# A graph network's first layer: its dense stages joined into one wave of fifteen steps over ten chunks

## The chip, the cores and the metric

The kernel runs on one core of a Trainium2 chip. The metric is the device time of one execution in microseconds; lower is better. A core has TensorE (PE; PEld is its weight load), VectorE (DVE), ScalarE (ACT), GpSimd (POOL), and DMA queues fed by SyncE (SP) and GpSimd.

## The reference, cut to what matters

Four graph layers follow each other on 5000 nodes of 128 features and 80000 edges, all in fp32. The change is in the first layer, which runs three times over the same weights:

```
for _ in range(3):
    att = _gat(x, src, dst, edge_attr, ...)          # edge attention: q(x[dst]), k and v (x[src]+edge_attr), softmax per node
    att = _ln(att @ w_ao.T + b_ao + x, ln1_g, ln1_b)
    inter = gelu(att @ w_int.T + b_int)              # 128 -> 512
    m = _ln(inter @ w_out.T + b_out + att, ln2_g, ln2_b)
    gi, gh = m @ w_ih.T + b_ih, h @ w_hh.T + b_hh
    r, z = sigmoid(ir + hr), sigmoid(iz + hz)
    n = tanh(inn + r * hn)
    h = (1.0 - z) * n + z * h
    x = _ln(h, ln3_g, ln3_b)
```

## The kernel before

State lies transposed in SBUF: features on the 128 partitions, 5120 padded nodes along the row, worked on in `CHUNKS` = 10 chunks of 512. The program is a list of blocks; in a block each engine has its own instruction list, in order, tied to the others by semaphores, and a block ends when all engines have ended. The first layer is a hardware loop over three iterations. In each: `node_rows` (L717 to L759) turns the state back into rows (4 transposes a chunk), stores them to `table_x` in DRAM and makes the queries in `t1`; `gat_score_pass`, `gat_softmax` and `gat_value_pass` go over the edges; then six dense blocks follow, each over all ten chunks before the next begins:

- `from_rows` (attention output): VectorE divides the sums by the softmax totals (L1520 to L1529), TensorE transposes (L1567), ScalarE copies, TensorE multiplies with `w_ao` (L1573), VectorE adds bias and residual (L1547).
- `layer_norm`, three times: TensorE sums over partitions with a matrix of ones (L624), VectorE centres (L686), ScalarE squares (L657), TensorE sums the squares by 128 columns against one column of ones (L631), ScalarE takes the root (L661), VectorE inverts (L691), TensorE spreads the result by transposes (L640), VectorE multiplies (L694), ScalarE applies gain and shift (L670). It works in two turns of five chunks and one root for each turn.
- `feed_forward`: four expansion products (L1587), Gelu on ScalarE (L1607), four contraction products in one bank (L1593), bias and residual on VectorE (L1614).
- `gru` (the gated update): six products a chunk (L1633 to L1636), two sigmoids (L1644, L1645), two VectorE steps (L1656, L1659), tanh (L1649), three more VectorE steps (L1663 to L1667).

ScalarE keeps its functions in tables; where the next function is in another table the compiler puts an ACT_TABLE_LOAD ahead of it. `clear_block` is an empty block that clears the semaphores before the loop goes round.

Of the kernel before, what the change touches and what calls it, by code (L numbers as in the profile page):

```python
# [17 lines left out]
F32 = mybir.dt.float32  # L18
I32 = mybir.dt.int32
ALU = mybir.AluOpType  # L20
ACT = mybir.ActivationFunctionType
AX_X = mybir.AxisListType.X

P = 128
N, E, D = 5000, 80000, 128
TILES = E // P
BLOCKS = -(-N // P)
# [25 lines left out]
Q_W = D + 4  # L53
CHUNK = 512
CHUNKS = NP // CHUNK
U = 5
BIG = 1.0e38
GAT_HEADS, GAT_ITERS, GAT_FF = 4, 3, 4
# [5 lines left out]
def bank4(ap):  # L64
    return ap.rearrange("p (a b) -> p a b", b=P)


def program(nc, io, out):
    ctx = ExitStack()
    with ctx:  # L70
        def sb(name, shape, dt=F32, where=ctx):
            return where.enter_context(nc.sbuf_tensor(name, shape, dt))

        def sems(*names):
            return [ctx.enter_context(nc.semaphore(n)) for n in names]
# [4 lines left out]
        @contextmanager  # L80
        def block(name, *used):
            with nc.Block(name) as b:  # L82
                cleared = [s for s in spent if s not in used]
                assert len(cleared) == len(spent), name
                spent.clear()

                @b.sync
                def _(sp):
                    for s in cleared:
                        sp.sem_clear(s)  # L90
                yield b
            spent.extend(used)

        def clear_block(name):
            with block(name):
                pass


        table_x = nc.dram_tensor("table_x", [NP, D], F32)
# [10 lines left out]
        ident = sb("ident", [P, P])  # L110
        iota_row = sb("iota_row", [P, P])
        ones = sb("ones", [P, P])
        (WK, WV, WQ, WAO, WINT, WOUT, GIH, GHH, GIN1, GIN2, WEDGE, GGIH, GGHH, NW) = (
            0, 1, 2, 3, 4, 8, 12, 15, 18, 19, 20, 24, 27, 30)
        wt = sb("wt", [P, NW, P])
        w3 = sb("w3", [P, 8, P])
# [10 lines left out]
        gate_bias = sb("gate_bias", [P, 2, 2])  # L127
        eps_col = sb("eps_col", [P, 1])
        blank = sb("blank", [1, P])
        bq_rows = sb("bq_rows", [P, D])  # L130
        bk_rows = sb("bk_rows", [P, D])
        bv_rows = sb("bv_rows", [P, D])
# [17 lines left out]
        hT = sb("hT", [P, NP])  # L150
        resT = sb("resT", [P, NP])
        t1 = sb("t1", [P, ACC_BLOCKS * Q_W])
        states = sb("states", [P, NP + ACC_BLOCKS * ACC_W])
        xT, acc = states[:, 0:NP], states[:, NP:]
        psum = ctx.enter_context(nc.psum_tensor("psum", [P, 8, CHUNK], F32))
# [4 lines left out]
        def wcol(name, k=0):  # L160
            return vec[:, VEC[name] + k:VEC[name] + k + 1]
# [4 lines left out]
        with ExitStack() as tmp:  # L166
# [25 lines left out]
            with block("constants", s_load, s_load2, s_const, s_wt, s_wcopy, s_xl, s_rows) as b:  # L192
                @b.sync
                def _(sp):
                    for to, of in loads[0::2]:
                        sp.dma_start(to, of).then_inc(s_load, 16)
# [342 lines left out]
        def at_least(eng, sem, value):  # L539

            if not (isinstance(value, int) and value <= 0):
                eng.wait_ge(sem, value)  # L542
# [27 lines left out]
        def acc_rows(c, lo, n):  # L570

            return acc[:, bass.ds(c * (4 * ACC_W), 4 * ACC_W)].rearrange("p (b w) -> p b w", w=ACC_W)[:, :, lo:lo + n]
# [5 lines left out]
        V = 2  # L578
# [23 lines left out]
        select = sb("select", [P, REGIONS, GROUP, P])  # L602
# [100 lines left out]
        r_stored = sems(*(f"rows_stored{u}" for u in range(V)))  # L703
# [126 lines left out]
        score = sb("score", [P, STEPS, GAT_HEADS])  # L830
# [745 lines left out]
        def feed_forward(name, src, dst, function, w_in, b_in, w_out, b_out):  # L1576
# [41 lines left out]
        g_product, g_gated, g_reset, g_new, g_read, g_step = sems(  # L1618
            "gru_products", "gru_gates", "gru_reset_applied", "gru_new", "gru_banks_read", "gru_step")

        def gru(name, msg, h, w_ih, w_hh, gates, b_in, b_hn):

            with ExitStack() as tmp:
                gate = sb(f"{name}_gate", [P, V, 2, CHUNK], F32, tmp)
                new = sb(f"{name}_new", [P, V, CHUNK], F32, tmp)
                with block(name, g_product, g_gated, g_reset, g_new, g_read, g_step) as b:
# [26 lines left out]
                    def _(dve):  # L1653
# [13 lines left out]
                            dve.tensor_tensor(h[:, cols(c)], new[:, u, :], gate[:, u, 0, :], ALU.add).then_inc(g_step, 1)  # L1667
                        pairs(dve, reset, update)

        b_stats, b_root, b_applied, b_scale, b_done = sems("bn_step", "bn_rooted", "bn_applied", "bn_product", "bn_done")  # L1670

        def batch_norm(name, src, gain, shift, dst=None, residual=None, weight=None, bias=None):
# [123 lines left out]
        def parts_of(w, first, count):  # L1796
            return [w[:, first + k, :] for k in range(count)]


        layer_norm("l0_norm", resT, xT, LN_EPS, also=hT)  # L1800
        with nc.Fori(0, GAT_ITERS) as it:
            node_rows("l0_rows", xT, queries=True)
            gat_score_pass("l0_scores", [it * ROWS] * REGIONS)
            gat_softmax("l0_softmax")
            gat_value_pass("l0_values")
            from_rows("l0_attention", t1, heads=GAT_HEADS, eps=1e-16, offset=bv_rows[:], weight=wt[:, WAO, :], bias=wcol("b_ao"), residual=xT)
            layer_norm("l0_ln1", t1, xT, 1e-12, wcol("ln1_g"), wcol("ln1_b"))
            feed_forward("l0_ffn", xT, t1, ACT.Gelu, parts_of(wt, WINT, GAT_FF), [wcol("b_int", k) for k in range(GAT_FF)],
                         parts_of(wt, WOUT, GAT_FF), wcol("b_out"))
            layer_norm("l0_ln2", t1, xT, 1e-12, wcol("ln2_g"), wcol("ln2_b"))  # L1810
            gru("l0_gru", xT, hT, parts_of(wt, GIH, 3), parts_of(wt, GHH, 3), gate_bias[:, 0, :], wcol("b_ih", 2), wcol("b_hh", 2))
            layer_norm("l0_ln3", hT, xT, 1e-12, wcol("ln3_g"), wcol("ln3_b"))
            clear_block("l0_end")
        add_state("l0_residual", xT)

# [57 lines left out]
```

## Time and profile before

| | us |
|---|---|
| median of 3 runs | 12100.61 (12093.36 to 12107.19) |
| the profiled execution | 12019.95 |
| its span | 12018.1 |
| busy in the span: TensorE, VectorE, ScalarE, GpSimd | 6550.1, 4612.7, 2251.5, 6209.6 |
| one iteration of the first layer, second | 1754.6 |
| its six dense stages, in the first | 256.7 |
| granted TensorE clock, mean | 0.734 |

The profile is of one execution, taken on the chip. A granted clock of 1 is 2.4 GHz for TensorE, of 0.5 it is 1.2 GHz. Busy times of engines overlap; what counts for a stage is the engine or the chain of waits that ends last in it. A row of the windows view has, in this order: the stretch, its length, the busy time and instructions of PE, PEld, DVE, ACT and POOL, the granted clock, the DMA share and GB/s. A row of the view by line has: busy us, mean ns of one, idle before, and what ended it.

### The profile page before, as it was taken

The numbers are of one execution on the slowest core, as the hardware profiler recorded it, in microseconds if no ns is written. First come the engines' busy times: TensorE is split into PE (matmuls) and PEld (weight loads), VectorE is DVE, ScalarE is ACT, GpSimd is POOL, SyncE is SP. The second block draws the span as 40 slices with busy tenths as digits, with TensorE's granted clock in tenths as the row PEclk, the third lists the DMA queues.
The fourth block names the chain that finished last, engine by engine and source line by source line (L and its number), as shares of the span: only waits on it lengthen the run. The fifth ranks groups of instructions, "written<-read, shape, count | busy, mean of one in ns | idle before, by whom it ended". The sixth has DMA issues, their size and how long they took to land. (4 is left out here: it accounts for less than half of the span.)

```text
span 12018.1 us, 148393 instructions
## 1 busy us (share of the span) xinstructions
PE 6550.1 (55%) x36272; PEld 5479.0 (46%) x36273; DVE 4612.7 (38%) x10118; ACT 2251.5 (19%) x4313; POOL 6209.6 (52%) x6365
## 2 busy tenths in 40 slices
PE   3666786566786665884335334433533443365555
PEld 3555665555765555853323223233323322244443
DVE  4444754444754444752113112211311221135555
ACT  1222552222542222641000000000000000011111
POOL 2666423666414665504663665466366456625553
PEclk6777898777897777996667666666766666677777
DMA  2444322444313443401111111211111121112221
GB/s 75 128 127 127 103 64 69 128 127 125 106 42 88 129 128 105 125 22 42 46 45 61 46 46 36 68 45 46 60 45 45 34 71 46 46 43 77 78 77 55
DMA packets 698434, 894.29 MB, mean 74 GB/s; under 512 B 148417, under 2 KB 443211, under 8 KB 698130
## 3 DMA queue, kind: packets, MB, share of 16 engines
q0 software_dynamic: 198368, 429.61, 13.6%
q1 hardware_dynamic: 498474, 461.96, 12.4%
q8 instruction: 51, 0.84, 0.0%
q14 instruction: 125, 1.02, 0.0%
q10 hardware_dynamic: 1416, 0.86, 0.0%
HBM read 698.72 MB, written 193.14 MB: 74 GB/s over the span
## 5 line engine op out<-in xcount | busy, mean ns | idle before, releaser
L857 POOL DMA_INDIRECT states<-table_typed,tile_idx x2512 | 2415.9, 962 | 1777.8 <-issue 721.2
L840 POOL DMA_INDIRECT states<-table_x,src_idx x2016 | 1980.1, 982 | 1862.7 <-POOLq L82 742.8
L979 PE MATMUL psum<-states,l_sums_select 128*128 x4480 | 905.5, 336 | 1729.7 <-issue 1696.3
L979 PEld LDWEIGHTS psum<-states,l_sums_select 128*128 128x128 f32 x4480 | 777.0, 244 | 1854.3 <-issue 1853.8
L961 DVE SCALAR_TENSOR_TENSOR l_sums_select<-dst_all,pair_start,iota_row 128x512 f32<-128x512 f32 x560 | 402.1, 749 | 2212.5 <-remote 1401.0
L1091 PE MATMUL psum<-ident,select 128*128 128x128 f32 x2016 | 418.3, 344 | 1199.3 <-DVE states L1059 723.4
L840 POOL DMA_INDIRECT l_pass_ring<-table_kv,src_idx x672 | 655.1, 975 | 658.9 <-DVE score L1312 286.3
L1068 DVE TENSOR_TENSOR states<-w,psum 128x512 f32<-128x512 f32 x504 | 345.2, 685 | 1544.0 <-ACT w L1048 969.0
L857 POOL DMA_INDIRECT states<-table_x,tile_idx x628 | 602.1, 959 | 626.2 <-POOLq L82 337.0
L979 PE MATMUL psum<-states,select 128*128 x2240 | 469.4, 348 | 808.8 <-issue 769.4
L944 ACT COPY t<-psum 128x512 f32<-128x512 f32 x50 | 29.3, 585 | 4534.1 <-PE psum L979 2586.3
L1091 PEld LDWEIGHTS psum<-ident,select 128*128 128x128 f32 x2016 | 297.9, 178 | 1263.5 <-DVE states L1059 567.3
L979 PEld LDWEIGHTS psum<-states,select 128*128 128x128 f32 x2240 | 404.7, 254 | 876.7 <-issue 876.0
L1144 POOL TENSOR_TENSOR w<-iota_row,dst_local 128x512 f32<-128x512 f32 x504 | 524.3, 1041 | 459.7 <-ACT select L1161 459.7
L1108 PE MATMUL psum<-t,l_scores_spread 128*128 x4032 | 675.2, 317 | 72.1 <-issue 71.6
L1105 PE MATMUL psum<-wt,l_scores_mixT 128*128 128x128 f32 x4032 | 713.5, 336 | 0.0
L1105 PEld LDWEIGHTS psum<-wt,l_scores_mixT 128*128 128x128 f32 x4032 | 672.1, 252 | 0.6 <-issue 0.2
L1108 PEld LDWEIGHTS psum<-t,l_scores_spread 128*128 128x128 f32 x4032 | 630.4, 233 | 75.8 <-issue 75.7
L961 DVE SCALAR_TENSOR_TENSOR select<-dst_all,pair_start,iota_row 128x512 f32<-128x512 f32 x280 | 200.2, 749 | 1035.7 <-remote 567.1
L1231 PE MATMUL psum<-l_values_msg,select 128*128 128x132 f32 x4032 | 549.5, 279 | 68.2 <-DVE l_values_msg L1171 68.2
L1048 ACT COPY w<-psum 128x512 f32<-128x512 f32 x504 | 300.5, 596 | 1355.7 <-remote 844.0
L1220 PE MATMUL psum<-wt,l_values_ring 128*128 128x128 f32 x4032 | 535.7, 277 | 15.4 <-DMA l_values_ring<-rows_dram 15.4
(357 smaller groups left out, 11997.4 us busy)
## 6 DMA issues: line engine op xcount, KB each, us to landing
states<-in_edge_attr_dram SPq DMA_DIRECT2D x2016, 64.0 KB
rows_dram<-l_scores_mixT SPq DMA_DIRECT2D x504, 256.0 KB
l_values_ring<-rows_dram SPq DMA_DIRECT2D x504, 256.0 KB
table_typed<-l_rows_rows SPq DMA_DIRECT2D x40, 1024.0 KB, 4.3
states<-table_typed,tile_idx POOLq DMA_INDIRECT x2512
states<-table_x,src_idx POOLq DMA_INDIRECT x2016
l_pass_ring<-table_kv,src_idx POOLq DMA_INDIRECT x672
table_x<-l_rows_rows SPq DMA_DIRECT2D x40, 256.0 KB, 2.3
```

The lines of the kernel that those rows point to most:

```text
L840: pool.indirect_dma_start(out=ring[:, k % REGIONS, u, :], out_offset=None, in_=table, in_offset=at).then_inc(gathered[k % REGIONS], 16)
L857: pool.indirect_dma_start(out=ring[:, k % TILE_RING, u, :], out_offset=None, in_=table, in_offset=at).then_inc(gathered[k % REGIONS], 16)
L961: dve.scalar_tensor_tensor(out=picked(k), in0=dst_all[:, bass.ds(column, GROUP)].unsqueeze(2).broadcast_to([P, GROUP, P]), scalar=pair_sta ...
L979: ins = pe.matmul(to, picked(k)[:, u, :], rows, start=False, stop=True, skip_group_check=True)
L1048: act.copy(key[:, r % 2, :, :], keys(r)).then_inc(p_evacuated, 1)
L1068: dve.tensor_tensor(prod.rearrange("p (a b) f -> p a b f", a=2), key[:, r % 2, :, :].rearrange("p (a b) f -> p a b f", a=2), queries(r)[:, ...
L1091: pe.transpose(psum[:, 0, u * P:(u + 1) * P], select[:, r, u, :], ident[:])
L1105: pe.matmul(keys(r)[:, u, :], mixT[:, r, u, :], wt[:, WK, :], start=True, stop=True)
L1108: ins = pe.matmul(queries(r)[:, u // pair, u % pair, :], spread[:, r % 2, u, :], q, start=True, stop=True)
L1144: pool.tensor_tensor(away[:, r % 2, :, :], iota_row[:].unsqueeze(1).broadcast_to([P, GROUP, P]), dst_local[:, bass.ds(step_of(i, r), GROUP ...
L1220: ins = pe.matmul(values(r)[:, u, :], ring[:, r, u, :], wt[:, WV, :], start=True, stop=True)
L1231: ins = pe.matmul(sums(r, u), select[:, r, u, :], msg[:, r, u, :], start=True, stop=True)
```

## The change

One block, `dense_chain`, takes the place of the six dense blocks and of `node_rows` in the loop. Its fifteen stages (TURN to NEXT) have fixed lags; in slot t a stage works on chunk t minus its lag, and there are 24 slots. All engines write their list out slot by slot, the latest stages first. What an engine has in a slot waits for the other engines' part of the same chunk, made in an earlier slot or this one. Each norm takes its root for one chunk at a time, into four columns. The three sums share bank 2, the spreads bank 4, the expansion and the gates banks 5 and 6. The expansions alternate between those two banks. The last stage, NEXT, is the rows and queries of the following iteration, so `node_rows` runs once ahead of the loop, with a `clear_block` of its own, and the third iteration makes rows that nobody reads.

The diff, with the helpers `here` (run a stage if its chunk exists), `due` (how many chunks a stage has done by slot t) and `reached` (wait if not yet waited for) and the other stages' bodies left out, and the stages' common indentation cut:

```diff
+            TURN, PRODUCT, SUM, VAR, SPREAD, EXPAND, CONTRACT, UPDATE, NEXT = 0, 1, (2, 7, 11), (3, 8, 12), (4, 9, 13), 5, 6, 10, 14
+            SLOTS = CHUNKS + NEXT
...
+            def next_rows(t, c):
+                reached(c_written[2], c + 1)
+                reached(c_mixed, due(t - 1, TURN))
+                reached(c_att, due(t - 1, PRODUCT))
+                reached(g_read, due(t - 1, UPDATE))
+                for k in range(4):
+                    pe.transpose(psum[:, 0, k * P:(k + 1) * P], xT[:, part(c, k)], ident[:])
+                for k in range(4):
+                    ins = pe.matmul(psum[:, 1, k * P:(k + 1) * P], xT[:, part(c, k)], wt[:, WQ, :], start=True, stop=True)
+                ins.then_inc(c_next, 1)
+            def summed(t, n, c):
+                reached((c_att, c_fed, g_step)[n], (c + 1) * (3 if n == 2 else 1))
+                for m in range(3):
+                    reached(c_centred[m], due(t if m > n else t - 1, SUM[m]))
+                pe.matmul(psum[:, 2, :], ones[:], norm_in(n, c), start=True, stop=True).then_inc(c_summed[n], 1)
+            def varied(t, n, c):
+                reached(c_squared[n], c + 1)
+                for m in range(3):
+                    reached(c_rooted[m], due(t - 1, VAR[m]))
+                for k in range(4):
+                    ins = pe.matmul(var_at(n, c, k), sq[n][:, c % 2, k * P:(k + 1) * P], ones[:, 0:1], start=True, stop=True)
+                ins.then_inc(c_varied[n], 1)
+            def spread(t, n, c):
+                reached(c_inverse[n], c + 1)
+                for m in range(3):
+                    reached(c_normed[m], due(t if m > n else t - 1, SPREAD[m]))
+                for k in range(4):
+                    ins = pe.transpose(psum[:, 4, k * P:(k + 1) * P], std[:, n, c % 2, k:k + 1].broadcast_to([P, P]), ident[:])
+                ins.then_inc(c_spread[n], 1)
+            def contract(c):
+                reached(c_fed, c)
+                for k in range(GAT_FF):
+                    reached(c_bent, GAT_FF * c + k + 1)
+                    ins = pe.matmul(psum[:, 7, :], wt[:, WOUT + k, :], inner[:, c % 2, k, :], start=k == 0, stop=k == GAT_FF - 1)
+                ins.then_inc(c_contracted, 1)
+            def gates_of(t, c):
+                reached(c_query, due(t, NEXT))
+                reached(c_att, due(t - 1, PRODUCT))
+                reached(g_read, c)
+                pe.matmul(psum[:, 1, :], wt[:, GHH + 2, :], hT[:, at(c)], start=True, stop=True)
+                reached(c_bent, GAT_FF * due(t - 1, EXPAND))
+                reached(g_gated, c)
+                for k in range(2):
+                    pe.matmul(psum[:, 5 + k, :], wt[:, GHH + k, :], hT[:, at(c)], start=True, stop=False)
+                reached(c_written[1], c + 1)
+                for k in range(2):
+                    pe.matmul(psum[:, 5 + k, :], wt[:, GIH + k, :], msg[:, c % 2, :], start=False, stop=True)
+                reached(c_next_copied, due(t, NEXT))
+                reached(c_mixed, due(t - 1, TURN))
+                pe.matmul(psum[:, 0, :], wt[:, GIH + 2, :], msg[:, c % 2, :], start=True, stop=True).then_inc(g_product, 1)
...
+            def expand(t, c):
+                reached(c_written[0], c + 1)
+                reached(g_gated, due(t, UPDATE))
+                for k in range(GAT_FF):
+                    reached(c_bent, GAT_FF * c + k - 1)
+                    pe.matmul(psum[:, 5 + k % 2, :], wt[:, WINT + k, :], att_in[:, c % 3, :], start=True, stop=True).then_inc(c_expanded, 1)
...
+            for t in range(SLOTS):
+                here(t, NEXT, next_rows, t)
+                here(t, SPREAD[2], spread, t, 2)
+                here(t, SUM[2], summed, t, 2)
+                here(t, CONTRACT, contract)
+                here(t, SUM[1], summed, t, 1)
+                here(t, SPREAD[1], spread, t, 1)
+                here(t, UPDATE, gates_of, t)
+                for n in (2, 1, 0):
+                    here(t, VAR[n], varied, t, n)
+                here(t, SPREAD[0], spread, t, 0)
+                here(t, SUM[0], summed, t, 0)
+                here(t, PRODUCT, attention, t)
+                here(t, EXPAND, expand, t)
+                here(t, TURN, turn, t)
+        @b.scalar
...
+            def gates_of(c):
+                act.wait_ge(g_product, c + 1)
+                at_least(act, g_step, 3 * c)
+                act.activation(gate[:, 0, :], psum[:, 5, :], ACT.Sigmoid, bias=gate_bias[:, 0, 0:1])
+                act.activation(gate[:, 1, :], psum[:, 6, :], ACT.Sigmoid, bias=gate_bias[:, 0, 1:2]).then_inc(g_gated, 1)
+                act.wait_ge(g_read, c + 1)
+                act.activation(new, new, ACT.Tanh, bias=wcol("b_ih", 2)).then_inc(g_new, 1)
+            def root(t, n, c):
+                for m in range(3):
+                    at_least(act, c_varied[m], due(t, VAR[m]))
+                at_least(act, c_spread[n], c - 1)
+                act.activation(std[:, n, c % 2, :], psum[:, 3, (n * 2 + c % 2) * 4:(n * 2 + c % 2) * 4 + 4], ACT.Sqrt,
+                               bias=eps_t[:], scale=1.0 / D).then_inc(c_rooted[n], 1)
+            def bend(c):
+                at_least(act, c_contracted, c - 1)
+                for k in range(GAT_FF):
+                    act.wait_ge(c_expanded, GAT_FF * c + k + 1)
+                    act.activation(inner[:, c % 2, k, :], psum[:, 5 + k % 2, :], ACT.Gelu, bias=wcol("b_int", k)).then_inc(c_bent, 1)
...
+            for t in range(SLOTS):
+                here(t, NEXT, next_copy)
+                here(t, SPREAD[2], written, 2)
+                here(t, SUM[2], square, 2)
+                here(t, SUM[1], square, 1)
+                here(t, SPREAD[1], written, 1)
+                here(t, UPDATE, gates_of)
+                for n in (2, 1, 0):
+                    here(t, VAR[n], root, t, n)
+                here(t, SPREAD[0], written, 0)
+                here(t, SUM[0], square, 0)
+                here(t, EXPAND, bend)
+                here(t, TURN, mix)
+        @b.vector
...
+            def feed(c):
+                dve.wait_ge(c_contracted, c + 1)
+                at_least(dve, c_centred[1], c - 1)
+                dve.scalar_tensor_tensor(out=fed[c % 2], in0=psum[:, 7, :], scalar=wcol("b_out"), in1=att_in[:, c % 3, :],
+                                         op0=ALU.add, op1=ALU.add).then_inc(c_fed, 1)
+            def make_rows(c):
+                at_least(dve, c_turned, c - 1)
+                at_least(dve, c_rows, c)
+                to = rows[:, c % 2, :].rearrange("p (b h e) -> p b h e", b=4, h=GAT_HEADS)
+                total = acc_rows(c, D, GAT_HEADS)
...
+            def update(c):
+                dve.wait_ge(g_new, c + 1)
+                dve.tensor_tensor(gate[:, 0, :], hT[:, at(c)], new, ALU.subtract).then_inc(g_step, 1)
+                dve.wait_ge(g_step, 3 * c + 1)
+                dve.tensor_tensor(gate[:, 0, :], gate[:, 0, :], gate[:, 1, :], ALU.mult).then_inc(g_step, 1)
+                dve.wait_ge(g_step, 3 * c + 2)
+                dve.tensor_tensor(hT[:, at(c)], new, gate[:, 0, :], ALU.add).then_inc(g_step, 1)
...
+            make_rows(0)
+            for t in range(SLOTS):
+                here(t, NEXT, query)
+                here(t, SPREAD[2], normed, 2)
+                here(t, SUM[2], centred, 2)
+                here(t, CONTRACT, feed)
+                here(t, SUM[1], centred, 1)
+                here(t, SPREAD[1], normed, 1)
+                here(t, NEXT, query_bias)
+                if t + 1 < CHUNKS:
+                    make_rows(t + 1)
+                here(t, UPDATE, reset)
+                here(t, SPREAD[0], normed, 0)
+                for n in (2, 1, 0):
+                    here(t, VAR[n], inverse, n)
+                here(t, SUM[0], centred, 0)
+                here(t, UPDATE, update)
+                here(t, PRODUCT, attended)
+            dve.memset(t1[:, BLOCKS * Q_W:], 0.0)
+        @b.sync
+        def _(sp):
+            for c in range(CHUNKS):
+                sp.wait_ge(c_next_copied, c + 1)
+                sp.dma_start(table_x[at(c), :].rearrange("(b p) f -> p b f", p=P), bank4(rows_out[:, c % V, :])).then_inc(r_stored[c % V], 16)
+            for stored in r_stored:
+                sp.wait_ge(stored, 16 * (CHUNKS // V))
...
         layer_norm("l0_norm", resT, xT, LN_EPS, also=hT)
+        node_rows("l0_rows", xT, queries=True)
+        clear_block("l0_start")
         with nc.Fori(0, GAT_ITERS) as it:
-            node_rows("l0_rows", xT, queries=True)
             gat_score_pass("l0_scores", [it * ROWS] * REGIONS)
             gat_softmax("l0_softmax")
             gat_value_pass("l0_values")
-            from_rows("l0_attention", t1, heads=GAT_HEADS, eps=1e-16, offset=bv_rows[:], weight=wt[:, WAO, :], bias=wcol("b_ao"), residual=xT)
-            layer_norm("l0_ln1", t1, xT, 1e-12, wcol("ln1_g"), wcol("ln1_b"))
-            feed_forward("l0_ffn", xT, t1, ACT.Gelu, parts_of(wt, WINT, GAT_FF), [wcol("b_int", k) for k in range(GAT_FF)],
-                         parts_of(wt, WOUT, GAT_FF), wcol("b_out"))
-            layer_norm("l0_ln2", t1, xT, 1e-12, wcol("ln2_g"), wcol("ln2_b"))
-            gru("l0_gru", xT, hT, parts_of(wt, GIH, 3), parts_of(wt, GHH, 3), gate_bias[:, 0, :], wcol("b_ih", 2), wcol("b_hh", 2))
-            layer_norm("l0_ln3", hT, xT, 1e-12, wcol("ln3_g"), wcol("ln3_b"))
+            dense_chain("l0_dense")
             clear_block("l0_end")
         add_state("l0_residual", xT)
```

## Rows read from the trace of the kernel before

**Rows 1.** Windows of the first iteration: attention, norm 1, feed-forward, gated update, gap, rows stage.

```profile
1664.90:1697.90 33.00, 19.98 (x60) 10.03 (x60) 29.16 (x60) 5.56 (x10) 0.00 (x0) 0.77 0.00 0
1698.20:1727.90 29.70, 26.27 (x140) 19.53 (x140) 13.95 (x23) 15.85 (x23) 0.00 (x0) 0.82 0.00 1
1727.90:1799.30 71.40, 70.41 (x160) 30.96 (x160) 7.49 (x10) 28.76 (x41) 0.00 (x0) 0.98 0.00 0
...
1829.10:1889.60 60.50, 53.43 (x120) 23.31 (x120) 33.86 (x50) 20.58 (x31) 0.00 (x0) 0.93 0.00 0
...
1921.60:1927.20 5.60, 0.00 (x0) 0.00 (x0) 0.03 (x1) 0.00 (x0) 0.00 (x0) 0.55 0.05 10
1927.20:1957.40 30.20, 17.31 (x120) 15.83 (x120) 23.46 (x41) 5.85 (x10) 0.00 (x0) 0.90 0.29 88
```

**Rows 2.** Timeline of TensorE, merged: start, us, what, count, idle before.

```profile
1698.20 4.53 PE L624 MATMUL psum<-t,ones 128*128 128x512 f32 x10 [1.11 <-PEq L82]
...
1706.95 6.24 PE L624 MATMUL psum<-t,ones 128*128 128x512 f32 x10
...
1714.15 2.40 PE L640 MATMUL psum<-ident,l_ln_std 128*128 128x128 f32 x20 [0.97 <-DVE l_ln_std L691]
...
1733.01 3.60 PE L1593 MATMUL psum<-l_ffn_inner,wt 128*128 128x512 f32 x8
...
1889.91 6.99 PE L624 MATMUL psum<-hT,ones 128*128 128x512 f32 x10 [7.31 <-PEq L82]
...
1910.56 4.53 PE L631 MATMUL psum<-ones,l_ln_sq 128*128 128x1 f32 x40
```

**Rows 3.** ScalarE's groups by line, first iteration: count, busy us, mean ns, idle before.

```profile
L1607 ACT ACTIVATE l_ffn_inner<-psum,vec 128x512 f32<-128x512 f32 x40 | 27.5, 687 | 39.0 <-PE psum L1587 39.0
L670 ACT ACTIVATE states<-states,vec 128x512 f32<-128x512 f32 x30 | 22.8, 807 | 9.9 <-DVE states L694 9.6
L657 ACT ACTIVATE l_ln_sq<-states 128x512 f32<-128x512 f32 x30 | 18.8, 630 | 33.2 <-DVE states L686 33.2
L1649 ACT ACTIVATE l_gru_new<-l_gru_new,vec 128x512 f32<-128x512 f32 x10 | 7.2, 720 | 4.6 <-DVE l_gru_new L1659 4.6
L1644 ACT ACTIVATE l_gru_gate<-psum,gate_bias 128x512 f32<-128x512 f32 x10 | 6.9, 687 | 31.9 <-PE psum L1636 31.9
L661 ACT ACT_TABLE_LOAD x3 | 3.8, 1283 | 0.1
L661 ACT ACTIVATE l_ln_std<-psum,l_ln_eps 128x20 f32<-128x20 f32 x6 | 1.7, 277 | 10.3 <-PE psum L631 10.3
```

**Rows 4.** VectorE's groups by line, the same stretch.

```profile
L686 DVE SCALAR_TENSOR_TENSOR states<-psum,t 128x512 f32<-128x512 f32 x20 | 13.8, 691 | 17.4 <-PE psum L624 17.4
L1614 DVE SCALAR_TENSOR_TENSOR t<-psum,vec,states 128x512 f32 (+1 forms) x10 | 7.5, 751 | 65.0 <-PE psum L1593 65.0
L691 DVE RECIPROCAL l_ln_std<-l_ln_std 128x20 f32<-128x20 f32 x6 | 1.6, 272 | 10.0 <-ACT l_ln_std L661 10.0
```

**Rows 5.** Timeline: two hops, a square before a load, two loads and what follows.

```profile
1699.33 0.69 DVE L686 SCALAR_TENSOR_TENSOR states<-psum,t 128x512 f32<-128x512 f32 x1 [1.04 <-PE psum L624]
...
1700.12 0.63 ACT L657 ACTIVATE l_ln_sq<-states 128x512 f32<-128x512 f32 x1 [4.58 <-DVE states L686]
...
1703.49 0.63 ACT L657 ACTIVATE l_ln_sq<-states 128x512 f32<-128x512 f32 x1 [0.23 <-DVE states L686]
1704.14 1.28 ACT L661 ACT_TABLE_LOAD   x1
...
1727.96 1.28 ACT L1607 ACT_TABLE_LOAD   x1 [0.27 <-PEq L82]
1730.08 0.69 ACT L1607 ACTIVATE l_ffn_inner<-psum,vec 128x512 f32<-128x512 f32 x1 [0.84 <-PE psum L1587]
```

**Rows 6.** Windows of two us: after a variance stretch, and in an idle of TensorE.

```profile
1886.00:1888.00 2.00, 0.00 (x0) 0.00 (x0) 1.93 (x4) 0.25 (x1) 0.00 (x0) 0.50 0.00 0
...
1708.00:1710.00 2.00, 2.00 (x3) 0.78 (x3) 0.69 (x1) 0.40 (x1) 0.00 (x0) 0.50 0.00 0
```

More of the change, by code:

```diff
@@ L1668, in _ @@
                         pairs(dve, reset, update)
+        c_rows, c_turned, c_mixed, c_product, c_att, c_link = sems(
+            "att_rows", "att_turned", "att_mixed", "att_product", "att_done", "att_rows_step")
+        c_summed, c_centred, c_squared, c_varied, c_rooted, c_inverse, c_spread, c_normed, c_written = (
+            sems(*(f"norm{n}_{what}" for n in range(3)))
+            for what in ("summed", "centred", "squared", "varied", "rooted", "inverse", "spread", "normed", "written"))
```

133 lines of the change are left out of this document (added).

## The prediction, made before the changed kernel was run

> **What bounds the kernel now.** I read the windows first, cut at the stage borders of the first iteration of layer 0 [rows 1]. From 1664.9, the end of the value pass, to the last norm's end at 1921.6 is 256.7 us; after 5.6 us for block ends, clear and loop, the rows stage takes 30.2, and then the next pass starts. GpSimd is idle in all of it, so only TensorE, VectorE and ScalarE can set its length. The feed-forward stage has TensorE busy 70.4 of 71.4 us at clock 0.98, and the gated update is near that; the attention and rows stages are held by VectorE (29.2 of 33.0, 23.5 of 30.2); the norms, of which one row stands for three, lie between, at clock 0.82. So the region is mostly TensorE-bound already; the longest waits in it are VectorE's for a contraction, 65.0 us [rows 4], and are cover rather than loss. Idle of other engines is no gain to be had.
>
> **TensorE's own work, the floor.** At 2.4 GHz a 512-column product is two passes of 0.43: ten passes take 4.53, eight (a contraction or an expansion) 3.43 to the next start [rows 2]. Twenty transposes take 2.40, so four 0.48; forty variance passes 4.53, so a chunk 0.90. Per chunk: product and three sums 4 x 0.86 = 3.4; expansion and contraction 6.9; six gate products 5.15; variances 2.7; four groups of transposes 1.9; next rows and queries about 1.3 (17.3 busy us for ten chunks, part at half clock [rows 1]). That is 21.4, or 214 us for ten. Against 256.7 + 30.2 = 286.9 now, perfect overlap would save 73 us an iteration.
>
> **What the wave costs, slot by slot.** All three engines go in written order, so a slot lasts as long as the longest round trip in it, not as long as TensorE's sum. Durations: Gelu, square and sigmoid 0.69, 0.63, 0.69, tanh 0.72, norm output 0.81, root 0.28 [rows 3]; a 512-column VectorE operation 0.69, feed 0.75, reciprocal 0.27 [rows 4]; a hop between engines 0.1 to 0.3: two passes begun at 1698.20 end at 1699.06, VectorE starts at 1699.33, ScalarE 0.10 behind it [rows 2, 5]. Roots, Gelu and sigmoid each come behind a table load of 1.28 [rows 3]. Now five loads serve an iteration. In the wave roots run in slots 3 to 21, Gelu in 5 to 14, sigmoid in 10 to 19, and ScalarE goes sigmoid, roots, Gelu in each: 35 loads. The load is not held by the wait behind it: it starts 0.02 after the last square and runs while the products that the root waits for go on [rows 5]. So the sigmoid's load hides under the products; those of the roots (from slot 10) and of Gelu stand on the round trip.
>
> Slots 0 to 5: VectorE bounds. make_rows is three full operations and two small ones of at most a reciprocal's length with their gaps, 2.55; centring, norm, inverse and attended add up to 2.4. By slot 5 its end is at 26.4; then square, load 1.28, Gelu, and since banks 5 and 6 alternate, expansions 2 and 3 only behind Gelu 0. Slot 5 ends at 30.7.
>
> Slots 6 to 9: contraction 3.43, feed to 4.46 behind it (and centring of norm 1), make_rows behind feed to 7.0, norm, inverse, centring to 8.7, square, load to 10.7, Gelu 0 to 11.4, two expansions 1.8, turn 0.5: 13.6. With the second norm's work 14.1, 14.6, 14.6. These are at 87.6.
>
> Slots 10 to 14: contraction, sum, transposes, gates: 9.9 to the gates' end. From there: sigmoids to 1.5, reset to 3.0, tanh 3.7, sqrt load 5.0, roots 5.8, inverse and centring 7.0, square 7.7, Gelu load 9.0, Gelu 0 9.7, two expansions 11.45. TensorE has 2.7 + 0.5 + 0.9 + 1.7 to do beside it and then stands about 4 us. With the sum, transposes and next rows that precede the next contraction (0.86, rising to 2.7) the slots are 22.2, 22.2, 21.5, 22.8, 22.2. At 198.5.
>
> Slots 15 to 19: no expansion, but norm 2's sum waits for the update, and VectorE does the update behind the inverses: 3.7 + 1.28 + 0.8 + three operations = 8.0 after the gates' end. So 17.9, 16.3 (the second sum waits for the first's centring), 14.5, 14.5, 13.9: at 275.6. Slots 20 to 23 and the last store: sum, centring, square, variance, root, inverse, transposes, norm, output, next rows, copy, DMA: 11.6. The whole, at full clock: 287.
>
> **The clock.** Ten 512-column passes take 4.53 us normally, 6.24 after a variance stretch and 6.99 after 7.3 us of idle [rows 2]; the granted clock is 0.50 in both places [rows 6], the lower of its two levels. A restart thus costs 1.7 to 2.5. Slots 16 to 20 begin after a gap as long as that: 5 x 2.5 = 12.5. Slots 10 to 14 have 2.7 us of variances and then the gap, but also 10 us of dense products: 0 to 1.7 each, I take 0.9, 4.5. Slots 1 and 5: 3. So 20, with bounds 5 (only half the late gaps count) and 45 (every slot from 5 on pays 2.5 or more). A chain is 307 to 308 us.
>
> **The rest.** Queries, their bias, copies and stores of next rows run in slots 14 to 23 beside the above; the queue of SP issues ten stores as before, 14 us apart, then 4, so ScalarE's copy does not wait for them. The third iteration makes next rows nobody reads; that is in its 11.6. Clearing and looping behind the chain replaces the 5.6 ahead of the rows stage, so they cancel. The rows stage ahead of the loop is the first iteration's own; the extra clear block is no row of its own, between 0 and the whole 5.6: I take 3. The three passes are untouched. Code written out straight already runs in the norms without a fetch gap in forty of them [rows 2], so 0.
>
> **The sum.** Goes: 3 x 256.7 + 2 x 30.2 = 830.5. Comes: 3 x 308 + 3 = 927. Difference +96.5. The profiled execution took 12019.95 (span 12018.1); the median of the runs is 12100.61, 80.66 higher, and I add the difference to that: 12197 us. The chain would have to be under 275.8 to pay. With the clock's bounds (292 and 333) and the hand-made round trips off by 10, likeliest case alone: 12120 to 12300.
>
> **The rivals.** *TensorE sets the slots (faster).* If neighbouring slots overlap better than I trace, the slots from 6 on last as long as TensorE's sum: 214 less 18 done before, plus 30.7 to get there and 8 to drain, is 235; 3 x 235 + 3 - 830.5 = -122, so 11978. For it: feed-forward and update now keep TensorE at 97 and 88% busy [rows 1]. Against it: there the two engines trade within one kind of work with no load between; here Gelu of a slot cannot start before the roots of the same slot. It decides once 32 of the 73 us from 308 down to 235 are gone. 0.18.
>
> *Nothing to see.* The clock costs nothing and the round trips are about ten us shorter, chain 268 to 284: within 24 us of 12101, which is the 0.2% that a measurement of this kernel can tell from no change. 0.12.
>
> *A switch of table costs more than its load.* After the load at 1727.96 the first Gelu starts 0.84 late, for which its product is an explanation too [rows 5]; if that were drain, some 20 loads an iteration stand on the path (slot 5 to 9 one, 10 to 14 two, 15 to 19 one): 17 us each, 50 in all, 12247. 0.10.
> The Trainium skill speaks against this change here: "ScalarE: Activation LUTs", section What ACT_TABLE_LOAD costs, gives 1283 ns plus about 1380 of drain for every switch, and its section on table sets asks for calls to be batched by set. The trace agrees with the 1283; of the drain it shows 0.02 before the load and at most 0.84 behind it. By the page's figure the sum would be 83 us longer, an estimate of 12280.
>
> *The clock stays low (slower still).* If every slot from 15 on ran wholly at 1.2 GHz (36 us of products on the path doubled, not 12.5 added) and slots 10 to 14 lost 5 each, the chain is 352: 12330. The attention stage speaks for it (TensorE busy 20 of 33 us, clock 0.77), the rows stage against it (17 of 30, clock 0.90) [rows 1]. 0.10.
>
> **The numbers.** My forecast holds 0.50, the two slower rivals 0.20, no change 0.12, faster 0.18. So slower 0.70, same 0.12, faster 0.18. Range for eight in ten: up to 12310, where most of the low-clock case is outside; down to 12020, part way into the faster case. Likeliest: 12197.
>
> **What the next profile would show.** Some 35 table loads an iteration, thirty or so of them more than now; TensorE idle 3 to 5 us in each of slots 10 to 14 with expansion 2 waiting for Gelu; 7 or 8 us between gates in slots 15 to 19 with the sum waiting for VectorE's update; slots of 14, 22 and 15 us; a chain of about 308, mean clock 0.8 or so. Wrong would be: ScalarE ahead of its products, slots of 18 us in the middle, or a chain under 276.

## The result, and where the time went

The changed kernel takes 12154.92 us (median of five runs, 12147.31 to 12166.59), the one before on the same chip 12100.61: a ratio of 1.0046, 95% interval 1.0031 to 1.0061, slower by 54 us (37 to 74). Forecast was 12197, range 12020 to 12310. Direction and range held, and so did the mechanism in the main (each slot waits for a round trip through ScalarE's table loads); the loss was forecast 42 us too large.

Two views of the profile after: the first lines of the page, and ScalarE's groups of table loads over the whole span, three iterations.

```profile
span 12152.2 us, 148055 instructions
PE 6604.6 (54%) x36392; PEld 5527.7 (45%) x36393; DVE 4627.7 (38%) x10195; ACT 2376.3 (20%) x4485; POOL 6206.1 (51%) x6365
...
L1872 ACT ACT_TABLE_LOAD x45 | 57.7, 1283 | 0.8
L1879 ACT ACT_TABLE_LOAD x30 | 38.5, 1283 | 0.5
L1863 ACT ACT_TABLE_LOAD x30 | 38.5, 1283 | 0.6
```

L1872 is the root, L1879 Gelu, L1863 the sigmoid: 105 loads, 35 an iteration, where the prediction had counted 35.

The span is 134 us longer than that of the profile before, which is more than the timed runs show. So the two spans were compared stretch by stretch. On VectorE's timeline, the wave begins with the first L1949, ends with L1999, and the next pass begins with L862; add_state, L2079, follows the third wave.

```profile
204.01 0.69 DVE L862 TENSOR_TENSOR select<-iota_row,dst_local 128x512 f32<-128x512 f32 x1 [1.09 <-PEq L82]
...
1684.84 0.17 DVE L1949 TENSOR_SCALAR l_dense_den<-states 128x16 f32<-128x16 f32 x1
...
1982.40 0.17 DVE L1999 MEMSET t<- 128x132 f32 x1
1990.38 0.69 DVE L862 TENSOR_TENSOR select<-iota_row,dst_local 128x512 f32<-128x512 f32 x1 [7.81 <-issue]
...
5252.59 0.18 DVE L1949 TENSOR_SCALAR l_dense_den<-states 128x16 f32<-128x16 f32 x1
...
5553.70 5.49 DVE L2079 TENSOR_TENSOR resT<-resT,states 128x5120 f32<-128x5120 f32 x1 [4.24 <-PEq L82]
```

The wave lasts 297.6 us and with the way to the next pass 305.5; before, those stages took 292.5 from 1664.9 to 1957.4 [rows 1], so +13.0. The second iteration took 305.6 instead of 294.0, +11.6. The third, which before had no rows stage behind it, ran from the same instruction to add_state in 301.1 instead of 261.7, +39.4: over half of the loss is the third iteration's rows, which nobody reads. The first pass starts 0.65 later. Together +64.7, within the interval of the timed 54. The other 69 us of the spans' difference lie in code that the change does not touch, and the first run below shows that they are not its doing.

Windows of the first wave, columns as in [rows 1]: slots 0 to 5, 6 to 9, most of 10 to 14, the late slots, and the whole.

```profile
1684.80:1715.00 30.20, 24.61 (x90) 13.53 (x91) 22.25 (x50) 14.31 (x22) 0.00 (x0) 0.85 0.00 1
1715.00:1773.00 58.00, 50.93 (x184) 26.73 (x183) 22.10 (x44) 32.51 (x48) 0.00 (x0) 1.00 0.00 0
1773.00:1880.00 107.00, 89.60 (x286) 46.58 (x284) 36.88 (x64) 56.45 (x79) 0.00 (x0) 0.87 0.01 3
1880.00:1965.00 85.00, 69.19 (x254) 41.77 (x255) 37.46 (x62) 40.24 (x57) 0.00 (x0) 0.83 0.05 16
1684.80:1982.60 297.80, 246.27 (x880) 138.95 (x880) 131.61 (x242) 149.81 (x215) 0.00 (x0) 0.88 0.03 9
```

The clock is full in slots 6 to 9; it is 0.85 ahead of them and 0.87 and 0.83 after them. The six stages of the kernel before had about the same clock as the wave as a whole:

```profile
1664.90:1921.60 256.70, 223.94 (x760) 123.09 (x760) 112.10 (x189) 102.03 (x151) 0.00 (x0) 0.89 0.00 0
```

With the rows stage TensorE was busy 241.3 of 286.9 us before, and 246.3 of 297.8 in the wave: the wave neither took idle time out of TensorE nor gained clock. In slot 12, in order of time, all engines:

```profile
1823.58 0.69 ACT L1863 ACTIVATE states<-psum,gate_bias 128x512 f32<-128x512 f32 x1 [2.15 <-PE psum L1795]
...
1826.39 0.72 ACT L1866 ACTIVATE states<-states,vec 128x512 f32<-128x512 f32 x1 [1.54 <-DVE states L1965]
1826.45 2.90 PE L1809 MATMUL psum<-l_dense_att_in,wt 128*128 128x512 f32 x4
...
1827.13 1.28 ACT L1872 ACT_TABLE_LOAD   x1
...
1828.42 0.57 ACT L1872 ACTIVATE l_dense_std<-psum,l_dense_eps 128x4 f32<-128x4 f32 x3
...
1828.88 0.82 ACT L1852 ACTIVATE l_dense_att_in<-t,vec 128x512 f32<-128x512 f32 x1
...
1829.71 1.28 ACT L1879 ACT_TABLE_LOAD   x1
...
1831.01 1.27 ACT L1879 ACTIVATE l_dense_inner<-psum,vec 128x512 f32<-128x512 f32 x2
...
1831.75 3.78 PE L1809 MATMUL psum<-l_dense_att_in,wt 128*128 128x512 f32 x4 [2.41 <-ACT l_dense_inner L1879]
...
1835.32 1.06 PE L1771 MATMUL psum<-ident,l_dense_std 128*128 128x128 f32 x4
...
1836.17 1.64 PE L1756 MATMUL psum<-hT,ones 128*128 128x512 f32 x2
```

This is the forecast chain: sigmoid, reset, tanh, load, roots, load, Gelu, expansion 2. Each load starts at the end of the activation before it (0.72 from 1826.39 ends at 1827.11) and the activation behind it follows at its end (1829.71 + 1.28 = 1830.99, Gelu at 1831.01). But in this slot TensorE's clock is down already at the first expansions (2.90 instead of 1.88) and stays down through the next (3.78 for four passes, transposes 1.06, a sum 1.64). In slots 11 and 13 the first expansions take 1.88 and only the pair behind the wait takes 3.78; in slot 10 that pair takes 2.57, in slot 14 1.98. Over the five slots this costs more than the prediction gave it.

### The profile page after: what moved, and what is told of

It reads as the page before. It is cut to its first block and busy times, and to the rows that moved or that the text cites. A ratio compares the mean times of both kernels' runs of the same rounds, so it can differ in the third digit from the quotient of the medians.

```text
span 12152.2 us, 148055 instructions
## 1 busy us (share of the span) xinstructions
PE 6604.6 (54%) x36392; PEld 5527.7 (45%) x36393; DVE 4627.7 (38%) x10195; ACT 2376.3 (20%) x4485; POOL 6206.1 (51%) x6365
## 3 DMA queue, kind: packets, MB, share of 16 engines
q14 instruction: 131, 1.07, 0.0%
## 5 line engine op out<-in xcount | busy, mean ns | idle before, releaser
L979 PE MATMUL psum<-states,l_sums_select 128*128 x4480 | 946.7, 345 | 1829.5 <-issue 1786.1
L979 PEld LDWEIGHTS psum<-states,l_sums_select 128*128 128x128 f32 x4480 | 811.5, 252 | 1962.2 <-issue 1960.4
## 6 DMA issues: line engine op xcount, KB each, us to landing
rows_dram<-l_scores_mixT SPq DMA_DIRECT2D x504, 256.0 KB
l_values_ring<-rows_dram SPq DMA_DIRECT2D x504, 256.0 KB
```

Of the source, the lines that this page charges most:

```text
L979: ins = pe.matmul(to, picked(k)[:, u, :], rows, start=False, stop=True, skip_group_check=True)
```

## The experiments

All ratios are to the kernel before, timed on the same chip as the run, with the 95% interval in brackets. Three of the kernels compute something else than the layer, to show what a load costs. "Chain" is the time from the first L1949 to the memset behind the last slot, first iteration, read from each run's trace as above.

**The kernel before, again.** No edit.

> The kernel before, unchanged, profiled on the same chip as the kernels beside it. Its profiled span was 12018.1 on another chip, the changed kernel's 12152.2: 134 us apart, where the timed medians are 54 apart. Theory: 53 of the 134 lie in the three score-softmax-value passes and 16 in the later layers, which the change does not touch, and belong to the chip and the execution, so here those stretches differ from the other kernels' by under 10 us in all. Rival: the wave's longer program slows the untouched passes; then they are again some 50 us shorter here than in the wave kernels beside it.

VectorE's timeline of this run, the first pass and the stretch behind it:

```profile
205.20 0.69 DVE L862 TENSOR_TENSOR select<-iota_row,dst_local 128x512 f32<-128x512 f32 x1 [0.32 <-PEq L82]
...
1683.94 0.25 DVE L1520 TENSOR_SCALAR l_attention_den<-states 128x16 f32<-128x16 f32 x2 [0.31 <-PEq L82]
...
1976.18 0.69 DVE L862 TENSOR_TENSOR select<-iota_row,dst_local 128x512 f32<-128x512 f32 x1 [0.32 <-PEq L82]
```

The first pass takes 1478.7 us here. In the other profile of the same kernel it took 1461.5, in the changed kernel 1480.8. The first iteration's dense stages took 292.2, against 292.5. So between executions of one and the same program the passes vary by 17 to 21 us an iteration, the dense stages by 0.3 in the first, 0.1 in the second and 3.8 in the third (257.9 here, 261.7 in the other profile). Over all three iterations the passes took 4439.0 here and 4437.4 in the changed kernel, and what follows add_state's start 6600.1 and 6598.5: the theory held, and the rival (a longer program slows the passes) falls. The span of this execution is 63.7 under that of the changed kernel.

**Gelu out, tanh in.**

```diff
-   act.activation(inner[...], psum[...], ACT.Gelu, bias=wcol("b_int", k))
+   act.activation(inner[...], psum[...], ACT.Tanh, bias=wcol("b_int", k))
```

> The changed kernel with tanh in place of Gelu in the wave's feed-forward (the function computed is another; the instruction has the same shape). Sigmoid and tanh then share their slot's table with it, so one load less stands on the path in each of slots 5 to 14, three times over. Theory that a load costs its own 1.28 and nothing else: 10 x 1.28 = 13 us an iteration, 38 in all, and up to 10 more if TensorE's shorter wait keeps its clock; about 12110 by the timed medians. Rival that every switch also drains some 1.4 us: twice that, 77 or more, 12078 or less. Rival that loads are hidden: no change.

Measured 1.0047 (1.0033 to 1.0060), chain 297.8: no change. This does not speak for hidden loads: the edit removed none. ScalarE's groups of the first wave in this run:

```profile
L1872 ACT ACT_TABLE_LOAD x15 | 19.2, 1283 | 0.3
L1879 ACT ACT_TABLE_LOAD x10 | 12.8, 1283 | 0.2
L1863 ACT ACT_TABLE_LOAD x10 | 12.8, 1283 | 0.2
```

I had overlooked that the roots stand between the gates and the feed-forward: sharing a table does not help where a third function lies between. So the run tells nothing of what a load costs; it does show that the chain repeats to 0.2 us.

**No table change at all.** As above, and:

```diff
-   act.activation(std[...], psum[:, 3, ...], ACT.Sqrt, bias=eps_t[:], scale=1.0 / D)
+   act.activation(std[...], psum[:, 3, ...], ACT.Identity, bias=eps_t[:], scale=1.0 / D)
```

> As the kernel with tanh for Gelu, and the roots' square root is replaced by a scaled copy as well, so the wave needs no change of table at all (it computes something else). Theory: of 35 loads an iteration about 30 stood on the path for the roots and Gelu, less those that hide under products: ten of Gelu in slots 5 to 14, ten of the roots in slots 10 to 19, six at most for roots in slots 5 to 9: 20 to 25 x 1.28 = 26 to 32 us an iteration, 77 to 96 in all, about 12060 to 12080, less up to 20 for the clock. Rival with a drain of 1.4 to each: 150 to 190, 11965 to 12005. Rival that TensorE sets the slots: under 20.

One load an iteration is left. Measured 0.9952 (0.9939 to 0.9966), so 0.94% or some 113 us less than the changed kernel; chain 253.9, 43.7 less. That is more than the 77 to 96 of the loads' own time by my count, within the 20 allowed for the clock, and less than the rival's 150. Slot 11, first a row of the changed kernel, then this run's; last, expansions 0 to 3 of slot 12 in this run:

```profile
1808.19 3.78 PE L1809 MATMUL psum<-l_dense_att_in,wt 128*128 128x512 f32 x4 [4.07 <-ACT l_dense_inner L1879]
...
1783.67 0.69 ACT L1863 ACTIVATE states<-psum,gate_bias 128x512 f32<-128x512 f32 x1 [3.46 <-PE psum L1795]
...
1786.50 1.88 PE L1809 MATMUL psum<-l_dense_att_in,wt 128*128 128x512 f32 x4
...
1789.60 1.98 PE L1809 MATMUL psum<-l_dense_att_in,wt 128*128 128x512 f32 x4 [1.22 <-ACT l_dense_inner L1879]
...
1791.42 1.02 PE L1756 MATMUL psum<-hT,ones 128*128 128x512 f32 x2
...
1805.23 5.29 PE L1809 MATMUL psum<-l_dense_att_in,wt 128*128 128x512 f32 x8
```

From sigmoid to expansion 2 are 5.93 us (8.79 in slot 11 of the changed kernel, from 1799.40), and the products run at full clock. The slot, contraction to contraction, shrinks from 24.5 to 18.7, of which two loads are only 2.6. What is left is either a drain that the rows do not show, or the clock. In slot 12 the clock is down here too (5.29 for eight passes; eight passes of a contraction take 3.60), with no wait of TensorE between the expansions.

**The loads stay, the idle time is filled.** TensorE writes products that nobody reads into bank 7: three ahead of expansion 2 in slots 10 to 14, and two in each slot from 16 to the last, 23 (the expectation says 16 to 20).

```diff
+   def fill(t, count):
+       reached(c_fed, due(t, CONTRACT))
+       for _ in range(count if t >= 10 else 0):
+           pe.matmul(bank4(psum[:, 7, :]), wt[:, WQ, :], wt[:, WINT:WINT + 4, :], start=True, stop=True)
...
    for k in range(GAT_FF):
+       if k == 2:
+           fill(t, 3)
...
+   if t > EXPAND + CHUNKS:
+       fill(t - 1, 1)
    here(t, NEXT, next_rows, t)
...
+   if t > EXPAND + CHUNKS:
+       fill(t - 1, 1)
    here(t, SUM[2], summed, t, 2)
```

> The changed kernel with products that nobody reads put where TensorE waits: three of 128x512 (six passes, 2.6 us at full clock) ahead of the third expansion in slots 10 to 14, one ahead of the next rows and one ahead of the third norm's sum in slots 16 to 20. TensorE waits 2.4 to 4.2 us there now, so they lie in idle time; all 35 table loads an iteration stay. Theory (half of what the loads cost is the clock that drops in the wait they cause: expansion 2 and 3 take 3.78 instead of 1.98, transposes 1.06 instead of 0.63, sums 1.64 instead of 1.02): slots 10 to 13 shrink by 2 to 3 us each, late ones by 1 each, 10 to 15 us an iteration, 30 to 45 in all, 12105 to 12125 by a before of 12100. Rival (the loads' own time is all, the clock was a by-product): no change, or a few us longer since the products end behind Gelu. Rival that the late slots' clock stays low anyway: only the middle part, 8 to 10 an iteration.

Measured 1.0018 (1.0009 to 1.0027), chain 281.7, 15.9 less, with all loads in place. TensorE in slot 12, and the window of the wave:

```profile
1801.84 1.88 PE L1816 MATMUL psum<-l_dense_att_in,wt 128*128 128x512 f32 x4
1803.56 2.74 PE L1744 MATMUL psum<-wt 128*128 128x512 f32 x6
1807.14 1.98 PE L1816 MATMUL psum<-l_dense_att_in,wt 128*128 128x512 f32 x4 [0.84 <-ACT l_dense_inner L1890]
1808.96 0.60 PE L1776 MATMUL psum<-ident,l_dense_std 128*128 128x128 f32 x4
...
1664.10:1946.00 281.90, 250.90 (x942) 136.58 (x942) 131.45 (x242) 149.42 (x215) 0.00 (x0) 0.98 0.03 10
```

More work makes the wave shorter: granted clock 0.98 instead of 0.88, slot 12 21.4 instead of 24.2, while sigmoid to expansion 2 takes the same 8.16 us in both. Of the 15.9, contraction 10 to contraction 15 gives 9.8 (118.7 to 108.8) and gates 15 to gates 19 gives 6.5 (65.8 to 59.2). The other 27.8 down to the kernel without loads are what 22 loads of 1.28 take, and the count of those on the path was 20. This split is rough: the kernel without loads has its clock at 0.95, so the loads may weigh some us more. Twenty drains of 1.4 on top of twenty loads would have made it 53.

**Only the roots' loads.** Gelu kept, ACT.Sqrt replaced by ACT.Identity as above; 12 loads an iteration remain.

> The changed kernel with the roots' square root replaced by a scaled copy, Gelu kept (it computes something else). The loads of the roots go, and with them Gelu's in slots 6 to 9 and the sigmoid's in 16 to 19; left are one of Gelu in slot 5, sigmoid and Gelu in each of 10 to 14 and one more sigmoid: some 12 an iteration of 35. Theory (each load on the path costs its 1.28, and those in slots 10 to 14 the clock besides): against the kernel without any load (chain 253.9) only Gelu's five in slots 10 to 14 stand on the path, chain 260 to 268. Rival that the roots' loads cost nothing and Gelu's all of it: above 280.

One execution was taken. Chain 267.8, at the upper end of the theory's range. Against the kernel without loads, slots 6 to 9 are the same to 0.01, since Gelu's table stays; slots 10 to 14 take 20.1, 20.1, 20.2, 22.7, 20.4 instead of 18.7, 18.7, 19.4, 19.7, 19.0: one load each and 1.7 more on the whole; slot 15 adds 3.3, with a sum that takes 2.08 instead of 1.46. So the roots' loads, with the 8 of Gelu and the sigmoid that go with them, bring 29.8 of the 43.7.

**Another order of the same steps.** TensorE's order within a slot (ScalarE and VectorE alike, with reset, tanh and update of a gate product in the slot behind it, and the waits fitted to the order):

```diff
 for t in range(SLOTS):
-    next_rows, spread 2, summed 2, contract, summed 1, spread 1, gates_of, varied 2 1 0,
-    spread 0, summed 0, attention, expand (all four), turn
+    contract, expand (0, 1), spread 2, next_rows, spread 1, spread 0, summed 1, expand (2, 3),
+    summed 0, attention, varied 2 1 0, turn, gates_of, summed 2
```

> The changed kernel's fifteen steps with the same lags between them, but each engine's order within a slot altered: contraction and first half of the expansion first, the second half behind the transposes and the first sum, the roots and the gates last, and the reset, tanh and update of a gate product moved into the next slot, under its contraction. All loads stay, but they now run while TensorE works. Theory (a slot is the longest round trip in written order): slots 10 to 14 last about 18 instead of 22 to 25, late slots 9 to 10 instead of 15 to 19, the chain 236 to 250 instead of 298: 150 to 186 less in all, 11920 to 11975 by a before of 12100. Rival (ScalarE sets the slots once its loads stand in a row: 3.8 of loads and 9.5 of work in slots 10 to 14 with Gelu behind them): slots stay at 21 or more, the chain above 275, 12060 or more.

Measured 0.9952 (0.9938 to 0.9965): 56 us less than the kernel before, some 113 less than the changed one. Chain 255.4, 5 above the bound expected. ScalarE behind the last expansion of slot 11, and the window of the wave:

```profile
1770.82 1.28 ACT L1878 ACT_TABLE_LOAD   x1
1772.12 0.42 ACT L1878 ACTIVATE l_dense_std<-psum,l_dense_eps 128x4 f32<-128x4 f32 x2
1772.55 1.28 ACT L1867 ACT_TABLE_LOAD   x1
1778.08 0.69 ACT L1867 ACTIVATE states<-psum,gate_bias 128x512 f32<-128x512 f32 x1 [4.24 <-PE psum L1798]
...
1662.60:1918.30 255.70, 227.61 (x880) 130.29 (x880) 133.28 (x242) 150.92 (x217) 0.00 (x0) 0.95 0.03 11
```

ScalarE waits 4.24 us behind two loads, so these two cost nothing. There are 37 loads an iteration instead of 35, and the chain is 1.5 us over that of the kernel without loads, so few can be on the path; slot by slot this was not read. Slots 10 to 14 last 18 to 21 instead of 22 to 25, the gates of slots 15 to 19 follow 10.8 to 12.9 apart instead of 14.7 to 19.1. It misses the expected 18 and 9 to 10: in slots 11 and 12 gate products behind the one-column products run at half clock, and in the late slots the reset, the next rows and the update take VectorE and TensorE in turn.

**The variance products set apart.** As the last, with varied 2, one gate product, varied 1, two gate products, varied 0.

> As e_order2, with the three groups of variance products (24 of one column behind each other there, 2.7 us, after which the next two gate products run at half clock: 3.02 or 2.58 and 2.06 instead of 1.98 and 1.02) set apart by gate products. Theory: the clock does not drop behind eight of them alone, slots 10 to 19 lose about 1 to 1.8 us each, the chain 240 to 246 instead of 255.4 and its mean clock above 0.97: 30 to 45 less than e_order2 in all, a ratio to before of 0.991 to 0.993. Rival: it drops later anyway, or the roots, which now come later, hold the next slot; then as e_order2, 0.995.

Measured 0.9948 (0.9934 to 0.9962), chain 256.0: the expectation fell. The half-clock products are indeed gone (four gate passes 1.96 instead of 3.02 or 2.58), and contractions 11 to 13 come 19.4 and 18.3 apart instead of 21.1 and 20.1. But slot 10 grew from 18.3 to 19.4, slot 13 from 18.9 to 20.6, and the late slots are the same to 0.02. The stretch of slots 10 to 14 is TensorE's: busy 89.5 of 95.6 us. Slots 10 and 13 gave back what 11 and 12 gained. TensorE in them:

```profile
1575.29 1.13 PE L1788 MATMUL psum<-hT,wt 128*128 128x512 f32 x2 [0.84 <-DVE t L1992]
...
1628.76 1.92 PE L1759 MATMUL psum<-l_dense_fed,ones 128*128 128x512 f32 x2
1630.47 2.65 PE L1816 MATMUL psum<-l_dense_att_in,wt 128*128 128x512 f32 x4
```

In slot 10 no variance products stand ahead of the first gate product any more, and it waits 0.84 for VectorE, which by the kernel's order has to read the attention product out of the same bank first (L1992). In slot 13 the clock is down later instead: a sum and two expansions take 1.92 and 2.65, where the order before had 1.02 and 1.88. That is the rival's case ("it drops later anyway") in one of the five slots, and with the 1.1 of slot 10 it is the whole of what was given back.

## Why the prediction was right, and where it was off

**The count of loads** held exactly: 35 an iteration.

**The round trips at full clock** held. Traced at 287; the kernel with filled waits, at a clock of 0.98, has 281.7. The parts, forecast without clock and measured in the changed kernel: slots 0 to 5, 30.7 and 27.1; 6 to 9, 56.9 and 54.1 (12.8, 13.6, 13.6, 14.2); 10 to 14, 110.9 and 118.7 (22.9, 24.5, 24.2, 25.3, 21.8; with the idle filled 108.8); 15 to 19, 77.1 and 83.3; the tail 11.6 and 14.4. The first slots were over-costed: make_rows was priced at 2.55 and repeats every 2.26 (first L1949 at 1684.84, second at 1687.10), which is at most half of the 3.6; the rest was not traced.

**The clock**, forecast at 20 with bounds 5 and 45, costs at least the 15.9 that the filled waits gave back. Its total was near and its split wrong: 4.5 was given to slots 10 to 14, which lose 9.8, and 12.5 to the late ones, which lose 6.5. One mistake was to take ten us of dense products in a slot as cover: behind the waits of 4.1 us in slots 11 and 13 the next four passes take 3.78 all the same. Another was to give each of slots 10 to 14 2.7 us of variance products: only in slot 12 do all three norms have theirs, the others have two groups. In slot 12 the first expansions, too, are at half clock behind the three groups (2.90), in the kernel without loads as well, whose waits are short; with the waits filled they take 1.88 behind the same products. So both waits and one-column products stand ahead of half clock, and how much each of them does was not separated. In the late slots the forecast took the way from gates to sum as one idle stretch like the 7.3 us before [rows 2]. It is as long as forecast, and its end waits for the update:

```profile
1893.78 1.02 PE L1795 MATMUL psum<-select,wt 128*128 128x512 f32 x2
...
1902.39 2.08 PE L1756 MATMUL psum<-hT,ones 128*128 128x512 f32 x2 [1.07 <-DVE hT L1973]
```

But of these 7.6 us TensorE idles only 3.0, in three pieces (1.28, 0.66, 1.07), with variance products, next rows and transposes between, and the slots lose about half of what was given them.

**The chain** is the term that was mis-sized: 308 forecast, 297.6 measured. In slots 0 to 5 3.6 less, and another 3 of clock given to slots 1 and 5; 2.8 less in 6 to 9; 3.3 more in the middle and 6.3 less in the late slots, their clock included; 2.8 more in the tail; and the forecast's own sum was 307.2 before it was rounded. Over three iterations (297.6, 297.5, 296.7) that is 10.4, 10.5 and 11.3, 32 us, the whole of the distance from +96.5 to the measured +64.7. That the likeliest value was no farther off is in part luck: errors of both signs in the parts cancel.

**The rest** cancels. The loop gap is 8.0 and 8.1 behind the wave instead of 5.6 ahead of the rows, 4.9 in two iterations; the second iteration of before was 1.6 longer than the first, which alone the prediction had read. The extra clear block was priced at 3, and the first pass starts 0.65 later; but in two executions of the kernel before it starts at 203.36 and 205.20, so the runs show no cost of it that is clear of their spread. Nor is the 64.7 exact: against the third iteration of the second execution of before, 257.9, it would be some 4 more. From 64.7 to the timed 54 is inside the interval. The prediction added its difference to the timed median and not to the span, and the first experiment bears that out.

**The rivals.** *TensorE sets the slots* falls for this order: it stands 1.3 to 4.2 us behind Gelu in every slot from 6 to 14. Its figure of 235 is not reached by the better order either (255.4), though there TensorE is busy 90.9 of 96.1 us in slots 10 to 14. *Nothing to see* needed a chain below 284. *A switch costs more than its load*: the Trainium skill, "ScalarE: Activation LUTs", section What ACT_TABLE_LOAD costs, adds about 1380 ns of drain to each switch. The trace disagrees: where nothing else is waited for, a load starts within 0.02 us of the activation before it, and the next activation within 0.02 us of the load's end. What the loads cost beyond their 1283 ns is TensorE's clock in the waits that they lengthen, and the products that nobody reads bought that back. *The clock stays low* had 352 for the chain; the clock dropped in the places named, by less.

## What to carry to other kernels

Joining stages into a wave pays only if each slot's dependent round trips shrink with it. Here slots 10 to 14, in which TensorE has about 18 us of work each (89.5 over the five in the last run), lasted 22 to 25, since gates, roots and Gelu of three different chunks were written one behind the other on ScalarE, each with its table. Write the order so that a table load follows the last use of the old table while TensorE has work queued: reordering the same steps was worth 42 us an iteration, 126 in all by the chain and 113 by the timed runs, where the wave had lost 65 and 54. An idle of TensorE can be charged twice, once as idle and once as half clock in the products behind it; look at both. Here waits of 4.1 us were followed by products at half clock, waits of 2.2 us in slots 6 and 7 were not, and one of 3.8 us in slot 14 was not either. And work that a wave takes into its last round for a next one that doesn't come is a cost of its own: 39 of the 65 us came in the third iteration.

## What the runs showed that I had not expected

Dummy products in idle time made the kernel 0.28% faster (1.0046 to 1.0018), 15.9 us of the first wave for 2.74 us of added products in each middle slot and two single ones in each late slot.

The chip and the execution move the untouched gather passes far more than the dense part. The kernel before took 12100.61, 12075.11, 12018.02 and 10643.27 us as the median on four occasions, while the chain of the reordered kernels was 255.4 beside the third and 256.0 beside the fourth. A difference of spans between two such occasions can't be put down to a change; the stretch that was changed can be compared.

A tanh behind a sigmoid needs no load (L1866 has none), yet with tanh in the feed-forward the sigmoid of the next slot still loads, in slots 11 to 14 too, where no root lies between (L1863, 10 loads in 10 slots). So two functions that share a table in one order need not in the other. From which table the tanh behind the roots is taken no row shows.
